# Both feed-forward fronts of a macaron layer rebuilt: norm and router of all groups first, then routing beside the shared feed-forward, with one written-out order for each engine

## What is computed

```
x = x + 0.5 * ffn(layernorm(x))
x = x + attention(layernorm(x))          # 4 heads of 128, one key/value head, rope, causal
x = x + 0.5 * ffn(layernorm(x))          # the same weights
```

```
logits = h @ gate_w.T                              # h: 4096 x 512, 32 experts
scores = sqrt(softplus(logits))
topk_idx = top_k(scores + bias, 6)                 # six experts for each token
topk_w = 1.5 * scores[topk_idx] / sum
pos = place of the token in its expert's queue     # a cumulative count over tokens
# tokens with pos >= CAP = 192 are dropped by that expert
routed = sum over the six of topk_w * (silu(h @ wg) * (h @ wu)) @ wd      # 512 -> 256 -> 512
shared = clip(silu(h @ sg.T) * (h @ su.T), -10, 10) @ sd.T                # 512 -> 256 -> 512
```

## Time and profile before

| | us |
|---|---|
| median of 3 runs (lowest, highest) | 1814.66 (1813.36, 1817.22) |
| the profiled execution, its own time | 1805.24 |
| its span, first to last instruction | 1803.5 |
| busy: PE, DVE, ACT, POOL | 1524.5, 1167.5, 991.7, 777.4 |
| mean granted clock of TensorE, of 1 | 0.943 |

### The profile page before, as it was taken

One profiled execution on the slowest core, in us unless ns is written; L12 is line 12 of the kernel. 1 busy time (PEld: TensorE's weight loads), 2 busy tenths in 40 slices (PEclk: granted clock), 3 DMA queues, 4 the chain that ended last, 5 costly groups with the idle time before them and its releaser, 6 DMA issues. The chain is left out here.

```text
span 1803.5 us, 27507 instructions
## 1 busy us (share of the span) xinstructions
PE 1524.5 (85%) x8626; PEld 1256.3 (70%) x8628; DVE 1167.5 (65%) x2369; ACT 991.7 (55%) x2038; POOL 777.4 (43%) x677
## 2 busy tenths in 40 slices
PE   4997766999998289999999999878986759999994
PEld 3775555877777267887887887656765548787773
DVE  5666676777776156666666665645676577777773
ACT  3334144777776156666666666533333146777773
POOL 3000163556554376556557655310000263656653
PEclk9998887999999689999999999998997888999998
DMA  6444314999996211111111111014444316899994
GB/s 214 150 146 165 117 35 140 264 259 264 264 264 174 66 42 41 48 36 59 42 42 59 36 42 41 25 62 141 154 146 141 108 39 211 260 261 262 264 265 85
DMA packets 87196, 244.98 MB, mean 136 GB/s; under 512 B 17649, under 2 KB 18609, under 8 KB 78673
## 3 DMA queue, kind: packets, MB, share of 16 engines
q1 hardware_dynamic: 64592, 192.12, 31.2%
q0 software_dynamic: 22528, 51.92, 13.7%
HBM read 175.25 MB, written 68.76 MB: 135 GB/s over the span
## 5 line engine op out<-in xcount | busy, mean ns | idle before, releaser
L1077 DVE TENSOR_TENSOR e_w_lo<-e_raw,e_w_hi 128x1024 fp32r<-128x1024 f32 x192 | 233.9, 1219 | 109.8 <-ACT e_w_hi L1001 91.7
L1001 ACT ACTIVATE e_w_hi<-e_raw 128x1024 fp32r<-128x1024 f32 x192 | 202.5, 1056 | 29.6 <-PEq L570 17.0
L1582 POOL TENSOR_SCALAR t_prob<-t_prob,t_inv 128x128 f32<-128x128 f32 (+7 forms) x128 | 111.8, 873 | 221.0 <-DVE t_inv L1489 221.0
L1156 PE MATMUL e_ps_gate<-e_xt,e_w_hi 128*128 128x384 f32 x512 | 164.7, 384 | 28.8 <-DVE e_w_lo L1077 28.6
L953 POOL DMA_INDIRECT e_xg<-htab,e_gather_idx x128 | 138.5, 1082 | 63.1 <-issue 42.8
L1156 PE MATMUL e_ps_up<-e_xt,e_w_hi 128*128 128x384 f32 x512 | 151.9, 361 | 0.0
L964 POOL DMA_INDIRECT x_after_ffn<-e_y,e_add_idx x64 | 102.4, 1600 | 110.6 <-DMA x_after_ffn<-e_y,e_add_idx 87.9
L964 POOL DMA_INDIRECT out<-e_y,e_add_idx x64 | 102.3, 1598 | 110.4 <-DMA out<-e_y,e_add_idx 88.2
L1384 ACT ACTIVATE t_prob<-a_wide,t_neg_max,a_q_scale 128x128 f32<-128x128 f32 (+7 forms) x128 | 106.4, 831 | 53.3 <-DVE t_neg_max L1483 53.1
L1157 PE MATMUL e_ps_gate<-e_xt,e_w_lo 128*128 128x192 f32 x512 | 132.9, 260 | 0.0
L1157 PE MATMUL e_ps_up<-e_xt,e_w_lo 128*128 128x192 f32 x512 | 129.4, 253 | 0.0
(11 more groups left out here) (318 smaller groups left out, 4644.7 us busy)
## 6 DMA issues: line engine op xcount, KB each, us to landing
e_raw<-in_w_experts SPq DMA_DIRECT2D x64, 1536.0 KB
htab<-d_h SPq DMA_DIRECT2D x16, 1024.0 KB, 4.2
d_x<-in_x SPq DMA_DIRECT2D x16, 512.0 KB, 5.0
q_x<-x_after_ffn SPq DMA_DIRECT2D x32, 256.0 KB, 3.2
t_res<-x_after_ffn SPq DMA_DIRECT2D x32, 256.0 KB, 2.6
x_after_attention<-t_res SPq DMA_DIRECT2D x32, 256.0 KB, 2.0
d_x<-x_after_attention SPq DMA_DIRECT2D x16, 512.0 KB, 5.4
x_after_ffn<-d_y SPq DMA_DIRECT2D x5, 1024.0 KB, 7.4
```

Of the source, the lines that this page charges most:

```text
L1001: act.activation(w_hi[u][:, cols], raw[u][:, cols], ACT.Copy).then_inc(hi_ready, 1)
L1077: dve.tensor_tensor(w_lo[u][:, cols], raw[u][:, cols], w_hi[u][:, cols].bitcast(F32), ALU.subtract).then_inc(lo_ready, 1)
L1156: pe.matmul(out, w[0][:, c, cols], xt[u][:, c, :, :], start=c == 0, stop=False)
L1582: pool.tensor_scalar(prob[:, u, 0:width(i)], prob[:, u, 0:width(i)], inv[:, u:u + 1], 1.0, ALU.mult, ALU.mult).then_inc(p_ready, 1)
```

## The change

`setup`, `dense_ffn` and `route` are gone; one block, `front`, does all of it.

- **Order.** All 8 groups pass norm, turning and router first. Behind the last logits comes routing. The shared feed-forward is cut into 48 pieces (16 gate, 16 up, 16 down: `piece`) that are laid between these steps: each engine's program calls `spot()` at fixed points, and a table per engine (`PE_AT`, `DVE_AT`, `ACT_AT`, `POOL_AT`, `SP_AT`) says at which point each piece stands. About three groups' gate and up and two groups' down stand among the norms, two and a half groups between the logits and the mask count, one group behind the count, and two groups between and behind the 32 tiles. The last down piece stands behind the last routing matmul.
- **Who does what.** `d_h` is written by ACT (four activations with scale and bias) and no longer by DVE; the clip and the low part of the inner product go to POOL for all 16 pieces (before: DVE for groups 0 to 4 both, in `route` the clip on DVE). In the table only the product with the partition's number is left, made by ACT; the tile's number comes from comparisons of the running count with the slot's number (L664 and L668, two of each). So a tile has 4 matmuls and not 8, and POOL has no part in it. The three sums of the logits are folded by a small matmul (`k.fold`) in place of a transpose.
- **Buffers.** Six places of `ht_hi`/`ht_lo` hold groups 0 to 5; x for the residual is loaded a second time, in tiles of 128 tokens through 6 buffers, 256 KB each, and stored from there.
- **Setup** is laid into group 0: its loads stand between those of x, ACT and DVE split the shared weights behind the first turning.
- **Attention's weights** are loaded and split in `routed_experts` of the first half: 10 chunks of 256 KB, six loads at its start and four later; POOL has a copy, a drain and a subtraction per chunk between a gather and an add.
- **Loops.** The front is straight code with no hardware loops.

The core of the diff:

```diff
-GA = 5
-HT_OF = {5: 1, 6: 0, 7: 2}
+PLACES = 6
+XS = 6
+PE_AT = (2, 4, 4, 4, 5, 5, 8, 9, 12, 13, 16, 17, 20, 21, 24, 25, 28, 29, 30, 31, 31, 31, 31, 31, 31, 31, 31, 31, 31,
...
+def piece(p):
+    g, r = divmod(p, 6)
+    kind = ("gate", "up", "down")[r % 3]
+    there = g > 0 if kind == "down" else g < G
+    return (kind, g - 1 if kind == "down" else g, r // 3) if there else (None, g, 0)
...
+            def spot():
+                for p in range(6 * G + 6):
+                    if table[p] == count[0] and piece(p)[0]:
+                        dense(*piece(p))
+                count[0] += 1
...
+                def dense(kind, g, b):                                    # GpSimd
+                    if kind == "up":
+                        i = FB * g + b
+                        pool.wait_ge(mul_done, i + 1)
+                        pool.tensor_scalar(inter[i % 2][:, :], inter[i % 2][:, :], SWIGLU_LIMIT, -SWIGLU_LIMIT,
+                                           ALU.min, ALU.max).then_inc(clipped, 1)
+                        pool.wait_ge(ihi_ready, i + 1)
+                        pool.tensor_tensor(in_lo[g % 2][:, b, :], inter[i % 2][:, :], in_hi[g % 2][:, b, :].bitcast(F32),
+                                           ALU.subtract).then_inc(ilo_ready, 1)
...
+                    for j in range(GT):                                   # ScalarE, normalise(g)
+                        got = act.activation(h[g % 2][:, j, :], x[g % 2][:, j, :], ACT.Identity,
+                                             bias=shift[g % 2][:, j:j + 1], scale=rstd[g % 2][:, j:j + 1])
...
+                for g in range(G):                                        # TensorE
+                    turn(g, 0)
+                    turn(g, 1)
+                    spot()
+                    if g:
+                        fold_logits(g - 1)
+                        spot()
+                    turn(g, 2)
+                    turn(g, 3)
+                    spot()
+                    router(g)
+                    spot()
+                fold_logits(G - 1)
+                spot()
                 pe.wait_ge(mask_done, 1)
...
-                        pe.matmul(out, of_group(tile_a[u]), b_of_group, start=False, stop=False)
-                        got = pe.matmul(out, of_group(part_a[u]), b_of_group, start=False, stop=last and g == GE - 1)
+                for t in range(NT):
+                    u = t % HOTS
+                    pe.wait_ge(hotb, t + 1)
+                    pe.wait_ge(ida, t + 1)
+                    for g in range(GE):
+                        got = pe.matmul(ps_tab[0:SA * EG, g * EG * SB_:(g + 1) * EG * SB_],
+                                        part_a[u][:, g, :, :].rearrange("p s e -> p (s e)"),
+                                        hot_b[u][:, :, g * EG:(g + 1) * EG],
+                                        start=False, stop=t == NT - 1 and g == GE - 1)
+                    got.then_inc(tabbed, 1)
+                    spot()
...
+                for e in range(4, 4 + chunks):                            # routed_experts, GpSimd
+                    gather_next(e // 2, e % 2)
+                    split_chunk(e - 4)
+                    scatter(e // 2 - 1, e % 2)
```

More of the change, by code:

```diff
@@ L173, in dense_ffn @@
-def dense_ffn(nc, a, k, n, src, acc, htab, logits, ht_hi, ht_lo):
+    at = SBUF_END - 4 * 2 * (WQKV + H * D)
+    for name, shape in (("wqkv", [P, KB, 6 * DH]), ("wo", [P, H, D])):
+        for part in ("hi", "lo"):
+            tensor = nc.alloc_sbuf_tensor_at(f"{name}_{part}", shape, F32R, offset=at)
+            at += 4 * shape[1] * shape[2]
+            if name == "wqkv":
+                k.wqkv_hi, k.wqkv_lo = (tensor, None) if part == "hi" else (k.wqkv_hi, tensor)
+            else:
+                k.wo_hi, k.wo_lo = (tensor, None) if part == "hi" else (k.wo_hi, tensor)
@@ L178, in dense_ffn, with front @@
+def front(nc, a, k, n, src, acc, accs, htab, slots, staged, raw, xs, w_loaded, y_stored):
     with ExitStack() as ctx:
@@ L498, in route @@
-def route(nc, a, k, n, src, acc, htab, logits, ht_hi, ht_lo, slots, raw, w_loaded, y_stored):
-    with ExitStack() as ctx:
-        sb = lambda name, shape, dt: ctx.enter_context(nc.sbuf_tensor(f"{name}{n}", shape, dt))
-        pb = lambda name: ctx.enter_context(nc.psum_tensor(f"{name}{n}", [P, 512], F32))
-        sem = lambda name: own_semaphore(nc, k, f"{name}{n}")
-        wide = [P, NT, E]
-        t1, t2, t3, t4, t5 = (sb(f"r_t{i}_", wide, F32) for i in range(1, 6))
-        score = sb("r_score", wide, F32)
@@ L508, in route @@
         seg = sb("r_seg", wide, F32)
-        mask = sb("r_mask", wide, BF16)
         bias = sb("r_bias", [P, E], F32)
@@ L593, in _, with load_x, store_h, load_xs @@
-                store(GA + 1)
+                def load_x(g):
+                    if g >= 2:
+                        sp.wait_ge(h_ready, g - 1)
+                    for m in range(2):
+                        sp.dma_start(x[g % 2][:, 2 * m:2 * m + 2, :], half(src, g, m)).then_inc(x_loaded[g % 2][m], 16)
+                def store_h(g):
+                    sp.wait_ge(h_ready, g + 1)
+                    sp.dma_start(group(htab, g)[:, :, 0:D], h[g % 2][:, :, :]).then_inc(h_stored[g % 2], 16)
+                def load_xs(i):
+                    if i >= XS:
+                        sp.wait_ge(y_stored[i % XS], 16 * (i // XS))
+                    sp.dma_start(xs[i % XS][:, :], tile(src, i)).then_inc(xs_loaded[i % XS], 16)
@@ new lines, in store_y @@
+                def store_y(i):
+                    sp.wait_ge(y_done, i + 1)
+                    sp.dma_start(tile(acc, i), xs[i % XS][:, :]).then_inc(y_stored[i % XS], 16)
+                    if 0 <= i - 1 and i - 1 + XS < NT:
+                        load_xs(i - 1 + XS)
+                def dense(kind, g, b):
+                    if kind == "down":
+                        store_y(4 * g + 2 * b)
+                        store_y(4 * g + 2 * b + 1)
+                spot = at_spots(SP_AT, dense)
@@ L604, in _ @@
+                act.wait_ge(lg_taken, G)
+                for u in range(2):
+                    act.wait_ge(h_stored[u], 16 * (G // 2))
+                act.activation(t2[:, :, :], logits[:, :, :], ACT.Abs)
                 act.drain()
@@ new lines, in router @@
+                def router(g):
+                    pe.wait_ge(t_lo, 4 * g + 4)
+                    if g:
+                        pe.wait_ge(lg_out, g)
+                    elif n == 0:
+                        pe.wait_ge(setup_lo, 1)
+                    at = place_of_group(g)
+                    for c in range(KB):
+                        for part, ht in enumerate((ht_hi, ht_lo)):
+                            got = pe.matmul(ps_lg[0:3 * E, :], k.router[:, c, :, :].rearrange("p s e -> p (s e)"),
+                                            ht[at][:, c, :], start=(c == 0 and part == 0),
+                                            stop=(c == KB - 1 and part == 1))
+                    got.then_inc(lg_ready, 1)
```

1049 lines of the change are left out of this document (466 added, 583 removed).

## The result

The changed kernel takes 1750.97 us (median of 4 runs, 1740.49 to 1754.33), the kernel before 1814.45 (1813.36 to 1817.22). The ratio is 0.9638, interval 0.9596 to 0.9680: faster by 3.6%, where 7.6% was forecast, and 33 us above the top of the range.

What follows compares the result with a forecast made beforehand. PE was taken to bound both fronts. Gains of 67.9 us in front 1 and 75.5 in front 0, less 5 in the experts, made 138.4; 1814.7 less that gave 1676 us, range 1656 to 1718.

Steps and rivals of the forecast that it cites:

- That wait is their cover: First-half experts: POOL's 2.9 us wait per add hides the chunks' copy and subtraction; 5 us taken for them and traffic.
- The start: Front 1, before PE has work: 10.8 us, plus 0.5 because ACT writes `d_h`.
- the tail: End of front 1, until the experts' gate starts: 10.9 us plus 0.7 for the last residual.
- TensorE's stretch: Front between start and tail: PE's work 171.3, losses 12.2 and chains 4, together 187.5 us.
- a term of 3.5 us: Front: folding of logits, mask's counts and last seven small matmuls, about 45 on PE, 3.5 us (2 to 6).
- the losses: Front: PE's time beyond its work, 12.2 us for waits and half clock, plus 4 for two serial chains.
- the forecast's two prices: Front, PE matmuls of 512 columns: 0.2333 us each for gate or up, 0.2267 for down.
- Its 7%: Front: PE's loss to waits and half clock, 9.3 us in the earlier second window, carried over as 12.2 of 171.3.
- rival 3: Fronts: PE loses less than in today's pipeline, 16 us less per front, 1644, half of that 1657; chance 0.10.
- The two chains: Front, last logits to mask and mask to first tile: uncovered 0 to 7 and 0 to 4, 4 us together.
- Rival 2: Fronts: DVE and POOL exclude each other and become the bound, 9 to 31 us more per front, 1694 to 1738; chance 0.22.
- Rivals 4 and 5: Fronts: SP's list stalls loads of x, slower than before, chance 0.03; time within 0.2% of before, chance 0.02.

Runs made afterwards that it cites:

- e1_wait: Changed kernel, with the drain between a weight chunk's copy and subtraction replaced by a wait for a semaphore the copy raises; 1699.82 us.
- e3_landed: e1_wait, with GpSimd waiting by named semaphore for the landed gathers between gather and add in ten second-half experts; 1772.15 us.
- e4_drain_ahead: e1_wait, with a drain put ahead of the gathers, behind the adds, in ten second-half experts; 1718.22 us.
- h1_loads_later: e1_wait, with the six loads of attention weights held back until TensorE has turned the first gathered rows; 1695.63 us.
- f5_no_fill_at_all: Changed kernel, with every shared feed-forward piece that stood behind the last logits moved behind the last tile on all engines; 1848.01 us.
- f4_pool_out: Changed kernel, with clip and low part of all 16 pieces of a front on VectorE instead of GpSimd; 1748.97 us.
- e2_drain_alone: e1_wait, with a drain between gather and add in ten second-half experts that split no chunk; 1775.83 us.

## Why the prediction was wrong

**The experts: the step that failed.** The prediction put it so: the chunks' copy and subtraction "stand between gather and add, where POOL waits 74.9 / 26 = 2.9 us for the last add to land. That wait is their cover", and took 5 us for them and for the traffic. It priced two of the three things that stand there. The third is the drain, which the description of the change names and for which the sum has no term. The drain measured 3.8 to 6.7 us of GpSimd's time each, 49.3 in ten experts, and the cover was spent on it: the last add had landed by the time the drain was through, as the next one waits only 0.16 us more. Without it (e1_wait) the stage is 10.2 us longer than before, against the 5 that were taken, within the bounds of that term. What the drain waits for is shown: e3_landed, which names the gathers, has the same time and the same gap, and in the changed kernel TensorE is released by the landed rows 0.16 us ahead of the subtraction. That adds in flight hold it as well is likely by e4_drain_ahead. The records of the gathers end at 345.84, so their ends in the timeline give no hint. The Trainium skill, page Perfetto Trace Analysis, section DMA Instruction — SWDGE (GPSIMD), states that such a record ends when the descriptors are generated and not when the data has moved. The trace agrees: TensorE gets these rows at 351.22, 5.38 us behind the end of the record.

**Front 1: right about the bound, 13.2 us short, and near by luck in one term.** The start (10.8 us, 11.3 forecast) and the tail (12.1, 11.6) hold. TensorE's stretch is 200.7, forecast at 187.5. The rows show three parts of this. First, the folding of the logits was part of a term of 3.5 us for "some 45" small matmuls; it alone has 64 matmul rows per front, and 8 of them take 1292.74 - 1291.85 = 0.89 us:

```profile
1291.85 1.05 PE L728 MATMUL d_ps_fold<-fold,d_lg_t 96*128 96x32 f32 x8
1292.74 0.48 PE L87 MATMUL d_ps_down<-shared_hi,d_in_hi 128*128 128x512 f32 x1
1293.06 0.39 PE L88 MATMUL d_ps_down<-shared_lo,d_in_hi 128*128 128x512 f32 x1
```

That is 7.1 us, and about 2.8 for the others by their starts, so the term is low by 6.4. Second, the losses, forecast at 12.2 + 4 = 16.2, are the 200.70 - 190.14 = 10.6 us in which TensorE isn't busy, and what the clock took in busy time, by the first and third of these windows:

```profile
1223.80:1240.00 16.20, 14.14 (x59) 0.66 0.97 343
1240.00:1360.00 120.00, 117.63 (x586) 1.00 0.52 173
1360.00:1380.00 20.00, 16.75 (x83) 0.83 0.56 184
```

14.14 x 0.34 + 16.75 x 0.17 = 7.7, an estimate. Together 18.3, 2.1 above the forecast. Third, the prices are a little low where kinds of matmuls alternate: the first of 512 columns behind the folding takes 1293.06 - 1292.74 = 0.32 us to the next start and not 0.23. Between 1240 and 1360, waits left out, one of 512 columns takes 0.238 us on average (0.231 by the forecast's two prices) and a transpose 0.107 (0.099). Over 576 and 128 of them that is about 5 us, which by this estimate is the rest.

The forecast's losses came near by luck. Its 7% is taken from the second window of the earlier trace rows, priced as 288 gate and up and 144 down matmuls, the work of six groups. The window has five groups' (the kernel before has groups 0 to 4 whole in `dense_ffn`, not 0 to 5). A group has 8 gate matmuls of each of L74 to L76, and the window shows 40:

```profile
L74 PE MATMUL d_ps_gate<-ht_hi,shared_hi 128*128 128x512 f32 x40 | 16.2, 404 | 0.0
```

By the same prices the work is 240 x 0.2333 + 120 x 0.2267 + 14.9 + 12.7 + 2 = 112.8 us, so 25.9 us of 138.7 were lost and not 9.3, 23% of the work and not 7%. Carried over, that would have been 39 us a front and a forecast of about 1730. What the new front lost is 18.3: TensorE loses less than in the old pipeline, which is rival 3's picture, and the miscount stood in for it.

**Front 0: 15.8 us short.** The transposes start at 14.9 (13.5 forecast), TensorE's stretch is 201.8 (187.5), the tail 15.7 (13.6: 11.6 + 2 for the six loads beside the first gather; the forecast's other 2 us, for the shared weights, belong to the stretch). The loads cost more than their 2 us: h1_loads_later took 3.8 from the tail.

**Filling TensorE's waits** was the right mechanism, and f5_no_fill_at_all shows it by its absence: what is laid behind the last logits is worth 49 us per front. That is no share of the 55 and 60 us that the change brought, since the kernel before filled with three groups there too. What the change brought in front 1 shows in the windows: between first transposes and tail TensorE was idle for 14.6 + 34.7 = 49.3 us and is idle for 10.6, which is 38.7 of the 55.9 us; the other 17.2 are busy time, with half the table matmuls and a granted clock that was 0.87 in `route`. The two chains that I left uncovered for 4 us are 40.5 us bare and 3.2 us covered.

**Rival 2**, VectorE and GpSimd as the bound, did not happen: 141.6 us busy of 200.7. The contention is there, 2.30 against 1.23 us for one instruction, and its sign in the prediction, longer `hot_a` rows, came true (0.417 against 0.351 us on average); but taking all pieces off GpSimd (f4_pool_out) was worth nothing that could be measured, and the clip alone 5 us in front 0. The Trainium skill, page GPSIMD Engine Reference, section Specifications, names this contention for VectorE instructions with two SBUF inputs; the trace agrees, as the stretched instruction has two. A rule about an engine's speed decides little where that engine is seldom waited for.

**Rival 3** is out by its number (TensorE lost no less than the 16.2 us of the forecast), though not by its picture, as said. **Rivals 4 and 5** are out: behind the start of front 1 VectorE waited 1.0 us for x, over two times, and the kernel is faster.

**The range** missed by the drain alone. The fronts' 29 us fit between 1676 and its end at 1718, in the room left for rival 2, and e1_wait, the changed kernel without the drain, measured 1700, inside it.

## What to carry to other kernels

In these runs, a drain on GpSimd behind indirect gathers was a wait for their landing (5.3 us on average, against 0.24 with none in flight). Where only one instruction's result is needed, let it raise a semaphore and wait for that. When a change puts work between two others, list every instruction of it, waits and drains first, and ask of each what is in flight on its engine at that moment.

Read the gain at the end of each stage, not at the end of the program: here 60 us were won and 59 lost again within the first half, and the total showed a smaller gain with no sign of where it went.

## What the runs showed of the hardware

Two things were new to me. First, TensorE's clock after a wait is not the same each time. Before the first tile of front 1 it waited 3.25 us in the changed kernel and ran the next 6 us at about half its full rate:

```profile
1369.00:1375.00 6.00, 5.92 (x18) 0.52 0.65 193
```

In e1_wait, the same instructions after 3.01 us of waiting:

```profile
1322.00:1328.00 6.00, 6.00 (x36) 1.00 0.59 179
```

x36 against x18 in 6 us. From the first table matmul to the first up matmul behind it, the same instructions take 6.56 us in the changed kernel and 3.93 in e1_wait: this alone makes 2.6 us between two executions of one front. The length of the wait doesn't decide it: e3_landed fell to 0.50 after 2.95 us, and e4_drain_ahead stayed at 1.00 after 3.03. These are the two long and the four short fronts 1 of the experiments.

Second, the experts have a slower rhythm in which they can stay. Behind the ten held-up experts of e2_drain_alone and e3_landed the rest kept to 11.5 to 12.5 us instead of 9.3, with nothing left of the cause; behind those of the changed kernel and of e4_drain_ahead they went back to about 9.3 within two or three. In this rhythm TensorE waits for nearly each gather (14 times, 37.7 us, between 1560 and 1725 in e2_drain_alone; 2 times, 2.3 us, between 1560 and 1690 in e1_wait). What decides between the two stays open.
